# Second attention: one score product between the two products for the exponentials, the other behind the value products

## The reference

```
q, k, v = split(x @ Wqkv)            # each (4, 512, 16 heads, 16)
q = q / (rms(q) + 1e-6) * scale_q ; k likewise     # one rms over the whole tensor
attn = softmax(einsum('bqhd,bkhd->bhqk', q, k))
z = einsum('bhqk,bkhd->bqhd', attn, v)
x = x + z.reshape(b, s, 256) @ Wo
```

## Time and profile before

| | us |
|---|---|
| median of 3 runs | 1879.54 (1879.35 to 1879.95) |
| the profiled execution, its own time | 1879.48 |
| its span, first to last instruction | 1877.70 |
| outside the span | 1.78 |
| S and T products side by side (14 groups) | 1129 to 1359 |
| PE busy in the span | 1530.3 (81%) |

### The profile page before, as it was taken

One profiled execution on the slowest core, in us unless ns is written; L12 is line 12 of the kernel. 1 busy time (PEld: TensorE's weight loads), 2 busy tenths in 40 slices (PEclk: granted clock), 3 DMA queues, 4 the chain that ended last, 5 costly groups with the idle time before them and its releaser, 6 DMA issues.

```text
span 1877.7 us, 14847 instructions
## 1 busy us (share of the span) xinstructions
PE 1530.3 (81%) x5080; PEld 693.7 (37%) x5080; DVE 1001.4 (53%) x944; ACT 625.2 (33%) x904; POOL 483.7 (26%) x137
## 2 busy tenths in 40 slices
PE   4888796667556776759988759888889999999998
PEld 3764343222222232325433312222235444444443
DVE  5993746999999999785433067676610000000000
ACT  1232553333333333221332215565542112122121
POOL 1994101665656656240112220000000000000000
PEclk7899897889999788868999969999988999999999
DMA  5000001221212221021010064111000000000000
GB/s 221 15 9 1 0 4 60 79 78 67 78 68 70 86 66 68 32 106 34 17 34 34 34 159 165 51 51 50 18 1 0 1 12 0 0 12 0 12 0 12
DMA packets 34860, 84.70 MB, mean 45 GB/s; under 512 B 5395, under 2 KB 21873, under 8 KB 34033
## 3 DMA queue, kind: packets, MB, share of 16 engines
q1 hardware_dynamic: 32881, 82.34, 13.1%
q10 hardware_dynamic: 1920, 1.57, 0.5%
HBM read 75.18 MB, written 8.65 MB: 45 GB/s over the span
## 4 chain that ended last, share of the span: by engine, by line
PE 53%; DVE 20%; DVEq 14%; issue 6%; ACT 3%; POOL 2%; ACTq 1%; DMA 1%; SPq 0%
PE ps L1124 12%; PE ps L1139 12%; DVEq L1595 10%; DVE arena L1591 8%; PE ps L996 3%; PE ps L908 3%; DVE mxs L1786 3%; PE ps L1036 2%; PE ps L976 2%; PE ps L950 2%; DVE arena L1486 2%; PE ps L729 2%; POOL arena L1895 1%; ACT arena L1411 1%; DVE arena L1597 1%
## 5 line engine op out<-in xcount | busy, mean ns | idle before, releaser
L804 PE MATMUL ps<-arena,early 128*128 128x512 f32 x512 | 272.1, 682 | 143.4 <-DVE arena L1597 143.4
L1917 POOL TENSOR_TENSOR arena<-arena 128x2048 f32<-128x2048 f32 x64 | 288.6, 4510 | 285.0 <-DVE arena L1573 137.0
L1591 DVE TENSOR_TENSOR_SCAN arena<-ps,arena 128x1024 f32<-128x1024 f32 x128 | 285.3, 2268 | 4.7 <-POOL arena L1917 4.7
L1296 ACT ACTIVATE ps<-arena,mam 128x511 f32<-128x511 f32 x256 | 166.2, 681 | 294.3 <-DVE arena L1591 286.8
L1124 PE MATMUL ps<-arena 128*128 128x512 f32 x512 | 241.7, 597 | 0.0
L1139 PE MATMUL ps<-arena 128*128 128x512 f32 x512 | 239.3, 592 | 0.0
L804 PEld LDWEIGHTS ps<-arena,early 128*128 128x128 f32 x512 | 107.1, 219 | 307.9 <-DVE arena L1597 189.6
L1453 ACT ACTIVATE arena<-ps,arena 128x512 f32<-128x512 f32 x128 | 87.9, 687 | 348.7 <-PE ps L1124 348.7
L1786 DVE TENSOR_REDUCE mxs<-ps 128x1 f32<-128x512 f32 x256 | 162.0, 684 | 73.9 <-PE ps L976 72.4
L1875 DVE SCALAR_TENSOR_TENSOR arena<-ps,b2s,arena 128x512 f32<-128x512 f32 x8 | 5.6, 746 | 334.4 <-PE ps L1139 334.4
L1411 ACT ACTIVATE arena<-ps,rho 128x1024 f32<-128x1024 f32 x128 | 140.4, 1110 | 88.6 <-PE ps L1036 88.4
(11 more groups left out here) (277 smaller groups left out, 1607.2 us busy)
## 6 DMA issues: line engine op xcount, KB each, us to landing
arena<-bc_scratch SPq DMA_DIRECT2D x64, 512.0 KB, 3.6
arena<-q_scratch SPq DMA_DIRECT2D x96, 64.0 KB, 2.1
arena<-in_cond SPq DMA_DIRECT2D x1, 5019.5 KB, 14.7
arena<-k_scratch SPq DMA_DIRECT2D x72, 64.0 KB, 2.1
arena<-in_dec_w SPq DMA_DIRECT2D x1, 3855.0 KB, 17.3
mam<-in_ids SPq DMA_DIRECT2D x4, 768.0 KB, 7.4
q_scratch<-arena SPq DMA_DIRECT2D x4, 768.0 KB, 3.3
k_scratch<-arena SPq DMA_DIRECT2D x4, 768.0 KB, 3.4
```

The lines of the kernel that those rows point to most:

```text
L804: last = pe.matmul(ps[:, m, :], ident, state[:, n % SLOTS, m, :], start=False, stop=(n == NS - 1))
L1296: last = act.activation(ps[:, DECAY + m, 1:S], dt[:, m, b * S + 1:(b + 1) * S], ACT.Exp, scale=a_neg[:, m * NS + n:m * NS + n + 1])
L1591: dve.tensor_tensor_scan(half, view(ps[:, DECAY + 2 * h, :], [[1, 2 * S]]), half, 0.0, ALU.mult, ALU.add).then_inc(s_scan, 1)
L1917: pool.tensor_tensor(state[:, n % SLOTS], du, view(b_rows[:, g % 2, n % G, :], [[0, M], [1, S]]), ALU.mult).then_inc(s_dbu, 1)
```

## The change

In each step of a group that has S products, S_2j stood behind Ta and Tb, and S_2j+1 followed it. Now S_2j stands between Ta and Tb, and S_2j+1 stands behind the V products of that step. In the steps with no V (0, 1, 3, 5 and 7) S_2j+1 keeps its place, third behind Ta. No instruction is added or taken away, and no other engine's order changes.

```diff
                         for i in (2 * pair, 2 * pair + 1):
                             last = pe.matmul(ps[:, 2 + 2 * pair + i % 2, :], kstack[0:STACK + 1, hg, i, kc * P:(kc + 1) * P],
                                              qstack[0:STACK + 1, hg, i, :], start=True, stop=True)
+                            if i % 2 == 0 and not (final and hg >= 2):
+                                scores(*ahead, 2 * j)
                         last.then_inc(s_t_mm, 1)
-                        if not (final and hg >= 2):
-                            scores(*ahead, 2 * j)
-                            scores(*ahead, 2 * j + 1)
                         if j % 2 == 0 and j:
                             values(b, hg, kc - 1)
+                        if not (final and hg >= 2):
+                            scores(*ahead, 2 * j + 1)
                         if j < 2 and hg == 1 and not first:
                             zn_columns(b - 1, j)
```

## The result

The changed kernel took 1885.98 us, median of 5 runs (1881.86 to 1888.90), against 1879.35 (1879.06 to 1879.95, 5 runs) for the kernel before: ratio 1.0034, 95% interval 1.0018 to 1.0051. The prediction was 1877.8 with a range of 1873.5 to 1882.5, so it had the wrong sign and missed. Two later comparisons of the same two kernels gave 1.0006 (0.9994 to 1.0019) and 1.0010 (0.9996 to 1.0024). In them the kernel before scattered too, 1876.78 to 1887.77 in the 32 runs of the first and 1877.41 to 1886.09 in the 23 of the second. So some 5 of the 6.6 us of the first comparison did not come back. This is the key to the case: both kernels carry some microseconds of TensorE clock that fall differently in each execution, and the first five runs of before happened to lie close together.

The account below looks back on a forecast made before the run. No engine was taken as full: TensorE waits in order, V_0 to V_2 behind S products held by maxima. Ordinary groups -4.2 and long ones +2.5 gave -1.7 us on 1879.48, so 1877.8, range 1873.5 to 1882.5.

Parts of the forecast that it names:

- The walk through the ordinary group: Step-by-step start times in one ordinary attention group: V blocks start sooner, and the group takes 14.62 us instead of 15.00.
- The ordinary term of the sum: Eleven ordinary groups, the first included, each 0.38 us shorter: 4.2 us gained.
- The first group: First attention group, under other starting conditions: taken like the other ordinary groups, a wrong value being worth tenths.
- The long groups: Three long groups: Tb 0.215 us later in four steps delays copies or V_3; 0.82 lost each, 2.5 us in all.
- The sum: Whole kernel: -4.2 us from ordinary groups and +2.5 from long ones, -1.7 us on 1879.48.
- the paragraph on the clock: Behind the attention: a shifted stretch could put one more or fewer block under the slow clock, 1.8 us either way.
- The range: Whole kernel: 1873.5 to 1882.5 us for 8 in 10, leaving out about 0.07 below and 0.11 above.
- the larger gain: Rival: long groups lose nothing or S_11 is not held, giving 1875.3 us or less; chance 0.24.
- S_11 is held: Ordinary group: S_11 waits for maximum 9 until 8.99 us, where a free one would start at 8.70.
- The wait inside the pair: Rival: Tb waits behind S_2j for its maximum, V_0 to V_2 gain nothing; +12 us, 1891.6; chance 0.14 beyond +3.8.
- Slower: Whole kernel more than 0.2% (3.8 us) slower, through VectorE's late maxima ahead of Tb; chance 0.14.
- nothing or a small loss: Whole kernel: a change between nothing and +3.8 us; chance 0.12.

Follow-up runs that it names:

- v_only: Against the kernel before: only the V block moved, ahead of S_2j+1, both T products left together; 1873.80 us, ratio 0.9958.
- long_old: Against the kernel before: new order in the ordinary groups alone, the three long groups in the order of before; 1879.10 us, ratio 0.9985.
- long_new: Against the kernel before: new order in the three long groups alone, ordinary groups as before; 1885.13 us, ratio 1.0023.
- pair_only: Against the kernel before: S_2j put between the T products, S_2j+1 left ahead of the V block; 1881.45 us, ratio 1.0003.
- before_tail: The kernel before plus two unread products per step in the last two groups (14 and 15); 1884.30 us, ratio 1.0018 to the kernel before.
- v_tail: V block moved alone plus two unread products per step in groups 14 and 15; 1875.34 us, ratio 0.9968 to the kernel before.
- before_fill: The kernel before with S_3, S_5 and S_7 of each long group made 3, 1 and 4 times more than needed; 1883.70 us, ratio 1.0010.

## Why the prediction was wrong

**The walk through the ordinary group held.** Every start came within 0.11 us of its forecast, in the order and with the causes forecast. The period is 14.72, not 14.62: I set 0.215 us from product to product. In the changed kernel it is 0.218 to 0.220 in an unbroken row and mostly 0.226 right behind a product that was held (S_2 at 1242.51, Tb at 1242.73). Over a group that adds 0.1 us. The ordinary term of the sum was -4.2 and came out at -3.1, first group included.

**The first group** was taken like the others, -0.4, and gave -0.3.

**The long groups held.** Forecast +0.82 each, measured +0.77, +0.77 and +0.72 at clock 1.00: 2.3 where the sum had 2.5. The delays of the three copies are 0.22 each, as one more product ahead of Tb makes them. The fourth, at V_3, is only 0.1, since the V block's move gives back 0.12 in a long group (v_only), where the prediction had 0.04. The Trainium skill, "TensorE: Matmul & The Clock Gate", section "Back-to-back issue gap", gives about 131 ns per product of 512 columns in a stream of loads and products, which would have made the term an estimated 1.6. The traces don't agree with that figure here: they have 0.22 per delay.

**The sum** of -1.7 us is -0.8 in the traces at clock 1.00. long_old confirms its first part by time (-2.8 us, with an interval from -4.7 to -0.9).

**What failed is the paragraph on the clock.** I gave it "1.8 us either way", behind the attention only, and let it weigh nothing in the chances. It should have been the widest term: in the profiled execution the clock cost 1.65 us in a long group and 3.4 behind the attention, against -0.8 for the whole change at full clock. Three things were missed. First, the long groups: the earlier trace rows shows TensorE waiting 1.01, 0.42 and 1.31 us within 7 us there, and the change lengthens each wait. Of the 15 long groups with the pair split, in five profiles (three of the changed kernel, long_new, pair_only), 6 had a slow stretch, at some 1.65 us each. Of the 15 unfilled ones with the pair together, 3 had one: 2 of 9 with the order of before (before, long_old, before_tail) and 1 of 6 with the V block moved alone (v_only, v_tail). With filling it was 0 of 12. In all nine groups that were caught the clock fell at the same place, from 0.20 us before to 0.30 us behind the end of the third wait. This fits the theory that TensorE's idling there lets the clock fall. But 6 of 15 against 3 of 15 proves no difference between the two orders, and before_fill gained nothing. Nor do the waits alone decide: groups with the same three waits were caught in one execution and not in the next.

Second, the stretches behind the attention. In three profiles of one kernel they add up to 30.8, 23.9 and 30.8 us, and over all fourteen profiles to 13.7 to 30.8. The time from the last V block to the end follows them closely: 488.4 us with 13.7 (v_tail), 490.1 with 17.1 (v_only), 491.7 with 20.5 (long_new), 493.2 with 23.9 (before), 496.6 with 30.8 (the changed kernel); the other nine lie within 0.1 us of these. That is half a microsecond per microsecond of slow clock. How long the first slow stretch lasts goes with where it begins. Beginning 0.6 to 0.7 us behind the end of the last V block it is 17.1 us long (two profiles), at 0.8 to 1.8 us 10.2 (six profiles), at 3.1 to 3.3 us 6.8 (two); in the other four it is missing, and only a later one comes. Nothing in the code sets this distance, since it differs between executions of one kernel.

Third, the stretch ahead of the attention. Its code is the same in every run, and still the first T product starts anywhere from 1128.05 to 1134.79 in the fourteen profiles. The stretches at clock 0.50 ahead of it add up to 265 us in one and to 331 in another. How much of these 6.7 us is clock was not tested, but they scatter any comparison by as much as the other two places do.

**The range** was built around runs of before that agreed within 0.6 us. I read that as "the clock repeats". It did not: 32 later runs spread over 11 us.

The rivals: the larger gain failed, since the long groups absorbed nothing and S_11 is held. The wait inside the pair is there, but with the size of the walk, not the +12 of the rival. "Slower" came true in the first comparison alone, by a mechanism to which I had given no sign. The two later ones, +1.1 and +1.9 us, fall into "nothing or a small loss".

What stays open: why the first five runs of before lay so close together; whether the new order truly meets the slow clock more often; and why filling took about 0.29% off the changed kernel (1.0008, the mean of the later two ratios, against 0.9979, that of the two filled ones), 5.5 us, where the slow stretches seen in its long groups explain some 1.7 us per execution.

## What to carry to other kernels

A walk through one period with distances read from the trace could here forecast an in-order engine to 0.1 us in 15; do it for each kind of period apart, since the same edit gained 0.28 in one and lost 0.77 in the other. Try the halves of such an edit singly: here, in an ordinary group, each gained more alone than both did together. And where a stretch runs with short waits on TensorE, or behind such a stretch, count the clock at either level as a term of some microseconds before reading a difference of 0.3% off a handful of runs.

## What the runs showed of the hardware

In nine of the thirty long groups without filling the granted clock fell from 1.00 (2.4 GHz) to 0.50 (1.2 GHz). It fell within 0.3 us of the end of the third of three waits, which were 1.45, 0.53 and 1.53 us in the changed kernel and 1.01, 0.42 and 1.31 in before_tail, spread over some 7 us. Over the whole group TensorE was still busy 19.31 of 23.70 us. The clock stayed at 1.00 in all twelve long groups whose waits were partly filled with products that nobody reads (the third wait was then 0.67 us in the changed kernel). Four such products of 512 columns cost no time when they stand where the engine waits anyway (22.06 with filling and without). Behind the attention each microsecond at clock 0.50 cost half a microsecond (488.4 us with 13.7, 496.6 with 30.8). A product that follows a held one starts 0.226 us behind it, against 0.215 to 0.220 in an unbroken row.
